# Gather and scatter in turns, a last stage opened by four DMAs, and two operations one slot later

## The chip, the cores and the metric

The kernel runs on one core of one Trainium2 chip. The metric is the device time in microseconds (us) of one execution. The core has TensorE (PE; its weight loads are listed apart as PEld), VectorE (DVE), ScalarE (ACT), GpSimd (POOL) and SyncE (SP), which only issues DMAs here. Each has its own instruction stream, and they meet at semaphores.

## The reference

Two transformer layers over x of shape [8, 512, 128] (4096 tokens), each sublayer followed by a normalisation without weights. What the change touches is the end of the first layer and all of the second:

```python
def _moe_forward(x, router_w, w_gate, w_up, w_down, ws_gate_up, ws_down):   # T=4096, E=64, K=8, C=64
    topk_w, topk_ids = jax.lax.top_k(softmax(x @ router_w.T), K)
    # every expert takes its first C=64 (token, choice) pairs
    xb = x_buf[:E * C].reshape(E, C, -1)
    h = silu(einsum('ecd,edf->ecf', xb, w_gate)) * einsum('ecd,edf->ecf', xb, w_up)
    y = einsum('ecf,efd->ecd', h, w_down).reshape(E * C, -1)
    routed = segment_sum(y[safe] * weight, tok, num_segments=T)
    return routed + silu(sg) * su @ ws_down

x = _layernorm(x + _L0_ffn_ref(x, ...))     # "r": 8 routed rows of a token are added, then normalised
x = _layernorm(x + _L1_attn_ref(x, ...))    # "a": normalises again, gated attention in groups of 32
x = _layernorm(x + _L1_ffn_ref(x, ...))     # "f": 8 experts, each on all tokens, top 2 weights; "t": its output
```

## The kernel before, in words

**First stage** (class `StageA`): for the 8 sequences in turn, attention, MLP and the router's logits. It writes the rows of all tokens, 128 features and 64 router weights each, to the DRAM table `token_rows`. Then DVE picks each expert's 64 tokens (`cand`, `slot_key`), while PE, ACT and POOL compute the shared expert of all tokens, and SP loads the late experts' weights.

**Expert stage** (in `build`): 32 turns `m`, each for two experts of 64 slots. All engines have it unrolled:
- POOL gathers the rows of 128 slots with one indirect DMA (`rows_all`, L1504). All 32 gathers stand ahead of all 32 scatters; from the ninth on each waits for the landing of the gather eight earlier.
- PE transposes them (L1680), ACT copies the transpose (`xgT`, L1590), PE does gate and up (`expert_up`, L1424), ACT the Silu (`sil`, L1406), DVE the product (`hexp`, L1635), PE the down projection (`expert_down`, L1434), DVE multiplies by the router weight into `y_all` (`expert_weigh`, L1414, drawn under the name `x1T_all`, whose memory it uses) and signals `y_sb`.
- POOL scatters the 128 result rows to the DRAM tensor `routed_rows` with one indirect DMA per turn (L1508), which waits for `y_sb`. `rows_scattered` counts landed scatters.

**Opening of the last stage** (class `StageC`). When all scatters have landed, SP loads the eight rows of each token of sequence 0, 2048 KB, with one DMA (`load_contrib`, L814) into `c`. DVE adds 1024 columns down to 128 in three steps over all four token blocks (L1011 to L1015), adds the shared part (`base_all`, L1018), and takes mean and variance (`stats`, L1000 and L1005). POOL then computes, one after another, rstd (add eps, a power, L827 and L829), y minus mean (L885), `x2` (L888), and from rstd the second factor `rq` (L891 to L897, the last a power). ACT makes `z` from `x2` and `rq` (L986), and PE starts on it. Meanwhile POOL corrects the weights `w1n` (L840 to L845: subtract the last column, put the bias there), PE transposes them (L1199), ACT rounds them to `w1_hi` (L915) and DVE keeps the rest in `w1_lo` (L1025).

**Last stage.** `bodies` (L780) runs ten passes. In a full pass, sequence `r` is summed, `a` gets its attention, `f` its eight experts, and `t` its output. A pass has sixteen slots `q`, in each of which PE does six matmuls of 512 columns for the experts (`up`), ACT a sigmoid (`sig`) and DVE a product (`unit`), and every second slot POOL adds one expert (`add_expert`, L837). `up(q)` waits for `unit(q-2)`. The rest stands in a slot by the table `AT`: within a slot it comes behind `up`, `sig` or `unit`. Seven passes have both `a` and `f`. At the end of `a`: `w` (output projection, slot 9) → statistics → rstd on POOL → `x3` (DVE, slot 10) → `x3T` (four transposes on PE, L1303; copies `x3h` on ACT and `x3l` on DVE) → `lg` (twelve small matmuls: the gating logits) → eleven small steps on DVE (`gating`, spread by the table `GATING`), which give the weights `comb` of the next pass.

## Time and profile before

| | |
|---|---|
| Time, median of 3 runs | 766.56 us (765.02 to 769.19) |
| Profiled execution, its own time | 763.75 us |
| Its span in the profile | 762.0 us |
| PE busy | 608.1 us, 80% of the span |
| PEld busy | 477.7 us, 63% |
| DVE busy | 432.4 us, 57% |
| POOL busy | 417.3 us, 55% |
| ACT busy | 276.7 us, 36% |
| Expert stage, first gather to last scatter landed | 186.2 to 299.3 us |
| Last stage | 299.3 to 762.0 us |

Busy shares are means over stages that have little in common. In the expert stage all engines work on small pieces and hand them round; in the full passes of the last stage PE is busy nine tenths of the time. The granted clock of TensorE is 0.5 in the one (the lower of its two levels, 1.2 of 2.4 GHz) and mostly 1.0 in the other. An idle time is worth reading by what ended it: the part behind `<-` in a row. "remote" there means that no instruction of another engine that the profile shows released it at that moment, and "issue" that the engine waited for nothing that is shown.

### The profile page before, as it was taken

The page shows a single profiled execution, that of the slowest core. Times are in us where ns is not written, and L with a number is a line of the kernel's source. Part 1 is how long each engine was busy: PE and PEld are TensorE (multiplying, and loading weights), DVE is VectorE, ACT ScalarE, POOL GpSimd, SP SyncE. Part 2 cuts the span into 40 slices and gives each one's busy share as a digit, 9 for nine tenths or more (in the row PEclk, how much of TensorE's full clock was granted, in tenths as well). Part 3 has the DMA queues.
Part 4 walks back from the last instruction along what each step waited for, and adds up shares of the span by engine and source line. Part 5 has one row for each costly group of instructions (what it writes and reads, how often), then busy time and mean ns, then how long its engine had stood idle before and what let it go on. Part 6 is the DMA issues. An engine that isn't in the chain of part 4 may idle for free.

```text
span 762.0 us, 10293 instructions
## 1 busy us (share of the span) xinstructions
PE 608.1 (80%) x3267; PEld 477.7 (63%) x3267; DVE 432.4 (57%) x1436; ACT 276.7 (36%) x561; POOL 417.3 (55%) x406
## 2 busy tenths in 40 slices
PE   5999995781516997276989989979899898998873
PEld 4888984341405875255777767757677677776652
DVE  2466786796103442633566766656657666575562
ACT  3456653251101222241525426235244362361320
POOL 5453352186773446625366665874857658434371
PEclk9999997595555555567899999999989999799996
DMA  4886755590320003330020210300303000000000
GB/s 113 193 294 249 283 223 233 140 234 11 80 79 25 32 29 104 141 111 1 18 93 1 77 48 1 125 1 0 124 0 105 19 1 15 0 15 1 0 15 14
DMA packets 46901, 61.89 MB, mean 81 GB/s; under 512 B 12835, under 2 KB 39556, under 8 KB 45828
## 3 DMA queue, kind: packets, MB, share of 16 engines
q1 hardware_dynamic: 44292, 56.08, 23.1%
q0 software_dynamic: 2560, 5.23, 2.4%
q8 instruction: 22, 0.36, 0.2%
q14 instruction: 27, 0.22, 0.1%
HBM read 35.10 MB, written 24.13 MB: 78 GB/s over the span
## 4 chain that ended last, share of the span: by engine, by line
PE 44%; DVE 21%; ACT 8%; issue 7%; POOL 6%; another core or an unknown queue 5%; DMA 3%; SPq 0%; DVEq 0%; POOLq 0%; ACTq 0%
PE pair L1189 5%; PE pair L1424 5%; PE pair L1191 5%; PE pair L1190 4%; DVE c_g L1058 3%; POOL c_acc L837 3%; DVE cand L1612 2%; PE pair L1434 2%; DVE keyT L1614 2%; PE pair L1297 2%; ACT c_sg L929 2%; PE pair L1284 2%; PE pair L1289 1%; PE pair L1680 1%
## 5 line engine op out<-in xcount | busy, mean ns | idle before, releaser
L837 POOL TENSOR_TENSOR c_acc<-c_acc,c_g 128x1024 f32<-128x1024 f32 x56 | 133.2, 2379 | 91.0 <-DVE c_g L1058 90.3
L1058 DVE SCALAR_TENSOR_TENSOR c_g<-pair,c_comb,c_sg 128x256 f32<-128x256 f32 x224 | 96.5, 475 | 65.9 <-ACT c_sg L929 63.6
L929 ACT ACTIVATE c_sg<-pair 128x512 f32<-128x512 f32 x128 | 76.1, 595 | 156.3 <-PE pair L1191 156.3
L1189 PE MATMUL pair<-c_w_hi,c_x3h 128*128 128x512 f32 x256 | 113.4, 443 | 7.5 <-DVE c_g L1058 6.2
L1190 PE MATMUL pair<-c_w_lo,c_x3h 128*128 128x512 f32 x256 | 104.5, 408 | 0.0
L1191 PE MATMUL pair<-c_w_hi,c_x3l 128*128 128x512 f32 x256 | 104.4, 408 | 0.0
L1189 PEld LDWEIGHTS pair<-c_w_hi,c_x3h 128*128 128x128 f32 x256 | 50.4, 197 | 24.4 <-DVE c_g L1058 14.9
L1191 PEld LDWEIGHTS pair<-c_w_hi,c_x3l 128*128 128x128 f32 x256 | 50.5, 197 | 12.3
L1190 PEld LDWEIGHTS pair<-c_w_lo,c_x3h 128*128 128x128 f32 x256 | 50.8, 198 | 7.9
L1508 POOL DMA_INDIRECT routed_rows<-x1T_all,dest_row x32 | 31.4, 982 | 40.4 <-DVE x1T_all L1414 37.8
L1635 DVE TENSOR_TENSOR hexp<-sil,pair 96x128 f32<-96x128 f32 x32 | 9.1, 284 | 67.5 <-ACT sil L1406 46.8
L1504 POOL DMA_INDIRECT rows_all<-token_rows,tok_row x32 | 30.5, 955 | 13.2 <-issue 9.4
L859 POOL TENSOR_TENSOR c_c<-c_c 128x2048 f32<-128x2048 f32 x7 | 32.0, 4576 | 0.3 <-DMA c_c<-routed_rows 0.3
L1424 PEld LDWEIGHTS pair<-xgT,wgu_late 128*96 128x96 f32 x160 | 30.1, 287 | 0.3 <-issue 0.3
L1414 DVE TENSOR_SCALAR x1T_all<-pair,rows_all 64x128 f32<-64x128 f32 x64 | 22.4, 350 | 11.4 <-remote 6.4
L1424 PE MATMUL pair<-xgT,wgu_late 128*96 128x64 f32 x160 | 28.8, 361 | 0.0
L1406 ACT ACTIVATE sil<-pair 96x128 f32<-96x128 f32 x32 | 8.7, 273 | 54.0 <-remote 27.0
L827 POOL TENSOR_TENSOR c_rs_f<-c_mv_f,c_eps 128x4 f32<-128x4 f32 x8 | 1.6, 202 | 45.4 <-DVE c_mv_f L1005 45.4
L1045 DVE SCALAR_TENSOR_TENSOR c_gateT<-pair,c_bcols,c_sgt 128x512 f32<-128x512 f32 x16 | 12.0, 749 | 24.7 <-ACT c_sgt L923 24.7
L1434 PE MATMUL pair<-wd_early,hexp 96*64 96x128 f32 x48 | 8.3, 448 | 22.1 <-issue 22.1
L1590 ACT COPY xgT<-pair 128x128 f32<-128x128 f32 x32 | 8.5, 265 | 47.3 <-PE pair L1680 33.5
L1424 PE MATMUL pair<-xgT,wgu_early 128*96 128x64 f32 x96 | 17.5, 364 | 9.1 <-ACT xgT L1590 7.0
(336 smaller groups left out, 1513.5 us busy)
## 6 DMA issues: line engine op xcount, KB each, us to landing
routed_rows<-rows_all SPq DMA_DIRECT2D x8, 2048.0 KB
c_c<-routed_rows SPq DMA_DIRECT2D x8, 2048.0 KB, 8.1
token_rows<-a_xw SPq DMA_DIRECT2D x8, 384.0 KB, 3.3
a_x<-in_L_attn_x SPq DMA_DIRECT2D x8, 256.0 KB, 3.1
base_all<-a_xw SPq DMA_DIRECT2D x8, 256.0 KB, 3.8
out<-c_outb SPq DMA_DIRECT2D x8, 256.0 KB, 5.4
wgu_late<-in_L_ffn_w_gate SPq DMA_DIRECT2D x4, 480.0 KB, 7.8
wgu_late<-in_L_ffn_w_up SPq DMA_DIRECT2D x4, 480.0 KB, 8.3
```

Source lines behind the costliest of these rows:

```text
L837: g.tensor_tensor(acc, acc, b[f"g{e % 2}"][:, :, :], ALU.add).then_inc(s["acc"], 1)
L859: g.tensor_tensor(c[:, :, 0:512], c[:, :, 0:512], c[:, :, 512:1024], ALU.add).then_inc(s["sum_step"], 1)
L929: a_.activation(b[f"sg{q % 2}"][:, :, :], self.pair[q % 2][:, :, H1:2 * H1], SIG).then_inc(s["sig"], 1)
L1058: ins = v.scalar_tensor_tensor(out=dst[:, j, :], in0=self.pair[q % 2][:, x, 0:H1], scalar=b[f"comb{uf}"][:, j * E1 + e:j * E1 + e + 1], in ...
L1189: t.matmul(dst, w_hi, x_hi, start=start, stop=False)
L1190: t.matmul(dst, w_hi, x_lo, start=False, stop=False)
L1191: return t.matmul(dst, w_lo, x_hi, start=False, stop=stop)
L1414: ins = nc.vector.tensor_scalar(y_all[part, m * D:(m + 1) * D], bank[4 + m % 2][part, 0:D], w, None, ALU.mult)
L1424: ins = nc.tensor.matmul(bank[2 + m % 2][0:F0, gu * P + h * CAP:gu * P + (h + 1) * CAP], wgu[:, h, gu, :], xgT[m % 2][:, h * CAP:(h + 1) * ...
L1434: ins = nc.tensor.matmul(bank[4 + m % 2][h * CAP:(h + 1) * CAP, 0:D], hexp[m % 2][:, h * CAP:(h + 1) * CAP], wd[:, h, :], start=True, stop ...
L1504: g.indirect_dma_start(rows_all[:, m * ROW:(m + 1) * ROW], None, table, bass.IndirectOffsetOnAxis(ap=tok_row[:, m:m + 1], axis=0)).then_in ...
L1508: g.indirect_dma_start(contrib, bass.IndirectOffsetOnAxis(ap=dest_row[:, m:m + 1], axis=0), y_all[:, m * D:(m + 1) * D], None, bounds_chec ...
```

## The change

Six edits:

1. The scatters are issued in turns with the gathers: eight gathers, then from turn 8 on gather `m` and scatter `m-8`, then the last eight scatters (`AHEAD = 8`).
2. The correction of `w1n` moves on POOL from behind the scatters to a place ahead of `setup_pool_scale`, before the experts; PE's transposes of it no longer wait for it turn by turn.
3. The first sequence's rows come in four DMAs of 512 KB, one per block of 128 tokens, each with its own semaphore, and DVE sums each block as it lands. Four of the eight `w1_lo` products go ahead of the sums, four behind the statistics.
4. `z` no longer hangs on `x2`: POOL computes `rq` and `nm` (minus mean times `rq`) directly from mean and variance, and ACT makes `z` from `y` with scale and bias. `x2` is computed behind that, and DVE's `w` slot waits for it. POOL waits for the last `z` before it writes `y` anew.
5. The load of sequence `r+1` waits for `y` of the first sequence instead of the third sum (one small addition later than the third sum).
6. `x3T` moves from slot 11 to 12, `lg` from 12 to 13, and the eleven gating steps from 2, 3, 3, 3 in slots 12 to 15 to 4, 4, 3 in slots 13 to 15.

```diff
-AT = dict(..., x3=10, x3T=11, lg=12, y=7, z=11)
-GATING = {12: (1, 2), 13: (3, 4, 5), 14: (6, 7, 8), 15: (9, 10, 11)}
+AT = dict(..., x3=10, x3T=12, lg=13, y=7, z=11)
+GATING = {13: (1, 2, 3, 4), 14: (5, 6, 7, 8), 15: (9, 10, 11)}
...
+    def setup_pool_w1(self, pool):
+        g, k, chain = self.nc.gpsimd, self.k, self.pool_chain
+        pool.wait_ge(self.w1_loaded, 16)
+        chain(g.tensor_copy(k["w127"][:, :], k["w1n"][:, :, D - 1]))
+        for q in range(4):
+            c = slice(8 * q, 8 * q + 8)
+            ins = g.tensor_tensor(k["w1n"][:, c, 0:D - 1], k["w1n"][:, c, 0:D - 1], bcast_last(k["w127"][:, c], D - 1), ALU.subtract)
+        chain(ins)
...
         sp.wait_ge(self.rows_scattered, 16 * EP)
-        self.load_contrib(sp, 0)
+        for j in range(NT):
+            sp.dma_start(self.b["c"][:, j, :], self.contrib_view[0][:, j, :]).then_inc(self.first_part[j][0], 16)
...
             if r is not None:
-                rstd("r", n, "rz_step", 7 * r + 1, "rz_step")
-                g.tensor_tensor(y3d, y3d, bcast_last(mv[:, :, 0], D), ALU.subtract).then_inc(s["rz_step"], 1)
...
+                pool.wait_ge(s["mv_r"], r + 1)
+                g.tensor_tensor(rs, var, k["eps"][:, :], ALU.add).then_inc(s["rz_step"], 1)
+                g.tensor_scalar(rq, var, 1.0 + EPS, EPS * EPS, ALU.mult, ALU.add).then_inc(s["rz_step"], 1)
+                g.tensor_scalar(nm, mean, -1.0, None, ALU.mult).then_inc(s["rz_step"], 1)
+                pool.wait_ge(s["rz_step"], 7 * r + 2)
+                g.tensor_tensor(rq, rq, k["mhalf"][:, :], ALU.pow).then_inc(s["rz_step"], 1)
+                pool.wait_ge(s["rz_step"], 7 * r + 4)
+                g.tensor_tensor(nm, nm, rq, ALU.mult).then_inc(s["rz_step"], 1)
+                g.tensor_tensor(rs, rs, k["mhalf"][:, :], ALU.pow).then_inc(s["rz_step"], 1)
+                g.tensor_tensor(x2, y3d, bcast_last(mean, D), ALU.subtract).then_inc(s["rz_step"], 1)
+                pool.wait_ge(s["rz_step"], 7 * r + 7)
+                g.tensor_tensor(x2, x2, bcast_last(rs, D), ALU.mult).then_inc(s["x2"], 1)
...
-                    act.wait_ge(s["rz_step"], 7 * r + 7)
-                    act.wait_ge(s["x2"], r + 1)
+                    act.wait_ge(s["rz_step"], 7 * r + 5)
...
+        dve.wait_ge(self.rows_scattered, 16 * EP)
+        for q in range(4):
+            w1_low(q)
...
+        for j in range(NT):
+            dve.wait_ge(*self.first_part[j])
+            v.tensor_tensor(c[:, j, 0:512], c[:, j, 0:512], c[:, j, 512:1024], ALU.add).then_inc(s["first_sum"], 1)
...
-            for m in range(EP):
+            def gather(m):
...
-            for m in range(EP):
+            def scatter(m):
...
+            for m in range(EP + AHEAD):
+                if m < EP:
+                    gather(m)
+                if m >= AHEAD:
+                    scatter(m - AHEAD)
```

On POOL in the expert stage, before: `rows_all<-token_rows` is a gather, `routed_rows<-x1T_all` a scatter.

```order
L1504 DMA rows_all<-token_rows,tok_row 128x192 x7
L1504 DMA rows_all<-token_rows,tok_row 128x192 [waits gathered0]
L1504 DMA rows_all<-token_rows,tok_row 128x192 [waits gathered1]
...
L1504 DMA rows_all<-token_rows,tok_row 128x192 [waits gathered7]
L1508 DMA routed_rows<-x1T_all,dest_row 32768x128 [waits y_sb] x32
L840 COPY c_w<-c_w1n 128x32 [waits c_w1_loaded]
```

And now:

```order
L1523 DMA rows_all<-token_rows,tok_row 128x192 x7
L1523 DMA rows_all<-token_rows,tok_row 128x192 [waits gathered0]
L1528 DMA routed_rows<-x1T_all,dest_row 32768x128 [waits y_sb]
L1523 DMA rows_all<-token_rows,tok_row 128x192 [waits gathered1]
L1528 DMA routed_rows<-x1T_all,dest_row 32768x128 [waits y_sb]
L1523 DMA rows_all<-token_rows,tok_row 128x192 [waits gathered2]
L1528 DMA routed_rows<-x1T_all,dest_row 32768x128 [waits y_sb]
```

From the tenth gather on, each now stands behind a scatter, and so behind a wait for the experts' results.

On POOL behind the first statistics of the last stage, before (`c_y` is y, `c_x` is `x2`):

```order
L827 TENSOR_TENSOR c_rs_r<-c_mv_r,c_eps 128x4 [waits c_mv_r,c_pad]
L829 TENSOR_TENSOR c_rs_r<-c_rs_r,c_mhalf 128x4 [waits c_rz_step]
L885 TENSOR_TENSOR c_y<-c_y,c_mv_r 128x512
L888 TENSOR_TENSOR c_x<-c_y,c_rs_r 128x512 [waits c_rz_step]
L891 TENSOR_TENSOR c_rq<-c_rs_r 128x4
L893 TENSOR_TENSOR c_rq<-c_rq,c_mv_r 128x4 [waits c_rz_step]
L895 TENSOR_TENSOR c_rq<-c_rq,c_eps 128x4 [waits c_rz_step]
L897 TENSOR_TENSOR c_rq<-c_rq,c_mhalf 128x4 [waits c_rz_step]
```

And now:

```order
L893 TENSOR_TENSOR c_rs_r<-c_mv_r,c_eps 128x4 [waits c_mv_r]
L894 TENSOR_SCALAR c_rq<-c_mv_r 128x4
L895 TENSOR_SCALAR c_nm<-c_mv_r 128x4
L897 TENSOR_TENSOR c_rq<-c_rq,c_mhalf 128x4 [waits c_rz_step]
L899 TENSOR_TENSOR c_nm<-c_nm,c_rq 128x4 [waits c_rz_step]
L900 TENSOR_TENSOR c_rs_r<-c_rs_r,c_mhalf 128x4
L901 TENSOR_TENSOR c_x<-c_y,c_mv_r 128x512
L903 TENSOR_TENSOR c_x<-c_x,c_rs_r 128x512 [waits c_rz_step]
```

ACT's `z` waited for the eighth of these rows and waits for the fifth now; the two wide ones are last.

On PE in a full pass around slot 12, before. `pair0` and `pair1` are the buffers of `up` in even and odd slots, `c_x30` is `x3`, `c_wg_hi` the first weight of the logits.

```order
L1191 MATMUL pair1<-c_w1_hi,c_x3l1 128x512
L1303 MATMUL pair3<-ident,c_x30 128x128 [waits c_x3]
L1303 MATMUL pair3<-ident,c_x30 128x128 x3
L1208 REGISTER_ALU
L1189 MATMUL pair0<-c_w1_hi,c_x3h1 128x512 [waits c_g]
...
L1191 MATMUL pair0<-c_w1_hi,c_x3l1 128x512
L1189 MATMUL pair3<-c_wg_hi,c_x3h0 128x8 [waits c_x3l]
```

And now:

```order
L1205 MATMUL pair0<-c_w1_hi,c_x3l1 128x512
L1318 MATMUL pair3<-ident,c_x30 128x128 [waits c_x3]
L1318 MATMUL pair3<-ident,c_x30 128x128 x3
L1221 REGISTER_ALU
L1203 MATMUL pair1<-c_w1_hi,c_x3h1 128x512 [waits c_g]
...
L1205 MATMUL pair1<-c_w1_hi,c_x3l1 128x512
L1203 MATMUL pair3<-c_wg_hi,c_x3h0 128x8 [waits c_x3l]
```

The six matmuls of slot 12 (`pair0`) stand ahead of the transposes now, and those of slot 13 (`pair1`) ahead of the logits.

## Rows read from the trace of the kernel before

**Rows 1.** Windows of the kernel before: busy time (and count) of each engine, clock, DMA.

```profile
218.00:222.00 4.00, 0.00 (x0) 0.00 (x0) 0.00 (x0) 0.00 (x0) 3.09 (x4) 0.50 0.31 82
...
238.00:294.00 56.00, 56.00 (x324) 44.95 (x323) 24.29 (x75) 13.19 (x49) 24.86 (x26) 0.50 0.09 30
...
456.00:504.00 48.00, 43.97 (x236) 34.55 (x234) 32.28 (x111) 20.64 (x40) 32.92 (x23) 1.00 0.15 50
...
504.00:555.00 51.00, 46.15 (x226) 36.56 (x227) 31.79 (x112) 20.26 (x38) 33.10 (x23) 0.92 0.14 47
```

**Rows 2.** Timeline of the expert stage: start, length, engine, operation, [idle <-releaser].

```profile
187.78 0.95 POOL L1504 DMA_INDIRECT rows_all<-token_rows,tok_row  x1 [0.30 <-issue]
...
194.23 0.71 DVE L1414 TENSOR_SCALAR x1T_all<-pair,rows_all 64x128 f32<-64x128 f32 x2
...
205.91 0.27 ACT L1406 ACTIVATE sil<-pair 96x128 f32<-96x128 f32 x1 [6.73 <-remote]
...
209.79 1.54 PE L1424 MATMUL pair<-xgT,wgu_early 128*96 128x64 f32 x8 [2.13 <-issue]
...
226.97 0.27 ACT L1406 ACTIVATE sil<-pair 96x128 f32<-96x128 f32 x1 [17.23 <-remote]
...
229.15 0.98 POOL L1508 DMA_INDIRECT routed_rows<-x1T_all,dest_row  x1 [0.30 <-issue]
...
235.37 0.27 ACT L1590 COPY xgT<-pair 128x128 f32<-128x128 f32 x1 [8.13 <-remote]
...
291.39 0.98 POOL L1508 DMA_INDIRECT routed_rows<-x1T_all,dest_row  x1 [1.28 <-DVE x1T_all L1414]
...
297.03 0.98 POOL L1508 DMA_INDIRECT routed_rows<-x1T_all,dest_row  x1 [0.30 <-issue]
```

**Rows 3.** A queue of the page's part 3: packets, MB, share of 16 engines.

```profile
q8 instruction: 22, 0.36, 0.2%
```

**Rows 4.** Timeline of the opening of the last stage.

```profile
299.31 29.41 SPq L814 DMA_DIRECT2D c_c<-routed_rows  x3
...
307.95 2.29 DVE L1011 TENSOR_TENSOR c_c<-c_c 128x2048 f32<-128x2048 f32 x1 [12.24 <-DMA c_c<-routed_rows]
...
312.26 0.69 DVE L1018 TENSOR_TENSOR c_y<-c_y,base_all 128x512 f32<-128x512 f32 x1
...
314.00 0.28 DVE L1005 BATCH_NORM_AGGREGATE c_mv_r<-c_st_r 128x2 f32<-128x6 f32 x3
...
314.70 1.05 POOL L829 TENSOR_TENSOR c_rs_r<-c_rs_r,c_mhalf 128x4 f32<-128x4 f32 x1
...
317.86 0.20 POOL L891 TENSOR_TENSOR c_rq<-c_rs_r 128x4 f32<-128x4 f32 x1
...
318.69 1.01 POOL L897 TENSOR_TENSOR c_rq<-c_rq,c_mhalf 128x4 f32<-128x4 f32 x1
...
319.79 1.28 ACT L986 ACTIVATE c_z<-c_x,c_rq 128x128 f32<-128x128 f32 x4 [0.68 <-POOL c_rq L897]
```

**Rows 5.** Timeline of GpSimd: the wait ahead of the experts, one w1n subtraction.

```profile
148.01 1.90 POOL L727 TENSOR_SCALAR c_whqk<-c_whqk,c_cols 128x640 f32<-128x640 f32 x1 [17.34 <-ACT c_bcols L776]
...
298.35 1.03 POOL L844 TENSOR_TENSOR c_w1n<-c_w1n,c_w 128x508 f32<-128x508 f32 x1
```

**Rows 6.** Waits of TensorE from 186 to 762 us: total, times, longest.

```profile
PE pair L1303 <- DVE c_x L1035: 19.7, 8, 4.9
```

**Rows 7.** Timeline of one pass of the last stage, at its end.

```profile
501.22 0.17 DVE L1074 MAX8 c_top<-pair 128x8 f32<-128x8 f32 x1
...
506.96 0.39 PE L1190 MATMUL pair<-c_w_lo,c_x3h 128*128 128x512 f32 x1
...
507.19 0.39 PE L1191 MATMUL pair<-c_w_hi,c_x3l 128*128 128x512 f32 x1
...
507.44 2.37 POOL L837 TENSOR_TENSOR c_acc<-c_acc,c_g 128x1024 f32<-128x1024 f32 x1 [0.96 <-DVE c_g L1058]
...
509.87 0.66 PE L1244 MATMUL pair<-ident,c_acc 128*128 128x128 f32 x4 [0.45 <-POOL c_acc L837]
```
## What the change was predicted to do

> **What bounds the kernel now.** I read the windows first: they show where no engine works. In the expert stage there is such a stretch: from 218 to 222 us PE, PEld, DVE and ACT did nothing at all, while POOL was busy with four gathers [rows 1]. From 238 to 294 us the same stage has PE busy for 56.00 of 56.00 us at clock 0.50 [rows 1]: there PE sets the pace. The full passes of the last stage are the third kind: PE 43.97 of 48 us at clock 1.00 [rows 1].
>
> Next I read the timeline of the expert stage, for what ends the idle time. POOL issues a gather every 1.25 us (0.95 busy, 0.30 between), from 186.5 us on, 32 of them, so to about 226.5 [rows 2]. The first turn's result is ready at 194.94 (194.23 + 0.71) [rows 2]. But then ACT comes late. A Silu starts at 205.91 after 6.73 us of idling; the matmuls that feed the next one end at 211.33, and it starts at 226.97, 15.6 us late and half a microsecond after the last gather. POOL then issues three scatters, the last until 230.13, and ACT is late once more, until 235.37 [rows 2]. All these rows say "remote": nothing that another engine did released ACT. From 235.4 on nobody is late any more, although scatters go on, one per 2.26 us (0.98 busy, 1.28 waiting for DVE) [rows 2]. So the pauses go with indirect DMAs issued without a gap, and about 36 us of the stage were spent in them. What the waiting engines lack is most probably their next instructions: they are the only thing outside the semaphores that they need, and they travel by DMA too, 22 packets in one queue of the page [rows 3]. A packet there is 16 KB (0.36 MB over 22).
>
> On this the Trainium skill has a rule: "Runtime: NRT & Kernel Launch", section "Instruction fetch mechanics", says that the sequencer streams its code by its own DMA queue and that this is mostly hidden. Packets of 16 KB agree with it; "hidden" does not fit the 15.6 us above, unless these pauses are no fetches. In that case the order of POOL's DMAs would change nothing in them; this is the rival "the pauses stay".
>
> At the opening of the last stage the timeline shows one chain: load issued 299.31, sums from 307.95, last sum ended 312.95, statistics ended 314.28, POOL's eight steps, `z` at 319.79 [rows 4]. In the full passes I read PE's waits: the four transposes of `x3` wait 19.7 us in 8 times, the longest 4.9 [rows 6].
>
> **Expert stage.** Nothing is added or removed on any engine: 32 gathers at 1.25 and 32 scatters at 1.28 us (0.98 + 0.30 [rows 2]), now mixed. POOL issues gathers 0 to 8 back to back, then pairs of 2.53 us. Three pairs later, near 205 us, it needs the result of turn 3. In the trace before, the Silu of that turn starts only at 205.91 [rows 2] (it is the fourth, at one per 2.26 us from the first result). So POOL has to fall silent, and with it the pauses should end, where before it went on for another 21 us. How soon ACT runs freely after that is not shown; the nearest rows give 0.5 us (gathers end, 226.97) and 5.2 us (230.13 to 235.37) [rows 2]. One round would put it at 205.5 to 210; if a scatter and a gather that slip in start the pause anew, two more rounds of 2.53 + 5.2 put it at about 225. I take 213, nearer to the single round. From free running to the last landing it took 299.3 - 235.4 = 63.9 us, set by PE at 2.26 us a turn; POOL's own share of that is 20 pairs and 8 scatters, 50.6 + 10.2 = 60.8 us, so it stays hidden by 3 us. The stage ends 235.4 - 213 = **22 us** earlier. Upper bound: no pause at all, first result 194.94, 31 turns of 2.26, then issue and landing of the last scatter, 3.6 us: 268.6, thus 30 us. Lower bound: the rivals.
>
> **Weights `w1n`.** POOL does the same subtraction, eight pieces of 1.03 us [rows 5], now as four of twice the size, about 8.5 us with a copy, where it waited 17.34 us for ACT [rows 5]. That wait hides it; without it the shared expert would start up to 8.5 us later. Behind the scatters it was beside the load of 8.6 us and cost nothing, so its going brings nothing.
>
> **Opening.** The load takes 8.6 us and the sums 5.0 [rows 4]. With four blocks, three quarters of the sums lie beside the rest of the load, since a block's sums (1.25 us, some 1.4 with four starts) are shorter than a block's share of the time (2.2). Behind the last block 1.4 us are left: **3.6 us** saved. Bounds: 2.6, if three more DMAs delay the last block by a microsecond, and 4. The four `w1_lo` products ahead of it are 2.8 us beside a load whose first block can't be there before.
>
> From the statistics to `z` it is 5.5 us (314.28 to 319.79). The new chain is three small steps, a power, one small step: a small step is 0.28 from start to start (317.86 to 318.69 are three), the power 1.05 [rows 4]. That is 2.2, with handing over 2.3: **3.2 us** saved, bounds 2.8 and 3.4. The wide steps to `x2` go behind it; they are needed at slot 9 of the next pass. The four `w1_lo` products behind the statistics (2.8 us) end before `zh` is there, and PE waits for them only at its first `up`. Both kept waits on `z` (POOL before it writes y, a slot-11 event of the pass before) find it long done: nothing. In later passes `z` was no one's last wait, so the shorter chain brings nothing there.
>
> **The slots.** Without the 4.9, the transposes wait 14.8 us in 7 passes, 2.1 each [rows 6]. Now PE has `up(12)` to do meanwhile: six matmuls at 0.23 us (506.96 to 507.19 [rows 7]), 1.39 us. `x3` is not later, so the logits end at the same instant as before (DVE reads them at 501.22 [rows 7]), with PE one slot further. What follows is the chain logits → gating → last products → POOL's last add at 507.44 → transposes of `acc` at 509.87 [rows 7]: 6.2 us from the logits to the add, in which three products of DVE stood; one of them is now ahead. A product is 0.9 us, and the gating steps in fewer slots give some of it back or not. I take **1.0 us** a pass, 7 in all. Bounds: 1.39 a pass (9.7), and minus 0.7 (-5) if the batches of four steps hold up products that PE waits for.
>
> **Clock.** The pass of 504 to 555 us took 51 us at a mean clock of 0.92 against 48 at 1.00 [rows 1]. PE stood still longest at the transposes; with a third of that gap left I expect fewer drops, and take **2 us**, between -3 and 6.
>
> **Sum.** 22 + 3.6 + 3.2 + 7 + 2 = 37.8 us off the profiled execution of 763.75 us: 726.0. The median of the runs is 2.8 above that execution, so 728.8; I say **728 us**. Half a per cent, 3.8 us, is about what a measurement of this kernel can tell from no change.
>
> **The rivals.**
> - *No pause at all* (chance 0.16): 30 us in the stage, 46 in all: 720 to 721; with the slots and clock at their best, 715. For it: before the third scatter everything is already less dense than before. Against: nine gathers still come without a gap, and the first late Silu lies right behind them.
> - *The pauses come back* (0.16): a pair of gather and scatter takes POOL 2.53 us where PE needs 2.26 a turn, so the indirect DMAs are again nearly without a gap, for 50 us instead of 40. Each time an engine needs code, it waits until POOL has run out of results, 5 to 7 us. Two or three more such pauses take 14 us back: 743.
> - *The pauses stay* (0.07): they hang on the place in the program, not on the gathers. The stage ends as before, 16 us are left: 751.
> - *The slots cost* (0.06): gating in fewer slots makes PE wait 1 us a pass more: 14 us less than forecast, 743.
> - *Slower* (0.07): fetches creep as long as any gather is in the queue, and now gathers last until the end. POOL then goes at the pace of pair plus quiet time, for 24 pairs. It decides against the change from 4.5 us a pair on: from 198 us, 24 x 4.5 and 10 us of last scatters and landing give 316, 17 later than before, which uses up the 16 us of the rest. At 5.6 us a pair the stage ends at 342, 43 us later: 794; at 2.53 + 5.2 it would be far more. Against it: scatters alone, 1.28 us apart from the next, did no harm.
>
> **How the numbers follow.** The forecast has 0.48, its own range is 722 to 737. The time holds in 715 to 750 about 8 times in 10 or a little more: it takes in every case but the slower one and some strays. Faster by over 0.5%: all but the last rival and 0.02 of others, 0.91; the same 0.02; slower 0.07.
>
> **What would show it.** Timeline of the expert stage: POOL's first gap near 205 us, ACT free by 210 to 216, no four-microsecond window without PE afterwards, the four first loads issued near 277. From the load's issue to the statistics' end 11.4 us instead of 15.0; from there to `z` 2.3 instead of 5.5. PE's waits: the transposes near 0.7 us a pass. The forecast is wrong if ACT's late starts go on behind 225 us, or if a full pass takes more than 47 us at clock 1.00.

## The result, and the profile after

| | before | after |
|---|---|---|
| Time, median of 4 runs each | 765.79 us (761.14 to 769.19) | 737.38 us (733.70 to 739.81) |
| Ratio | | 0.9629, 95% interval 0.9558 to 0.9700 |
| Profiled execution, span, mean clock | 763.75, 762.0, 0.845 | 739.48, 737.4, 0.862 |
| Until the first gather | 186.2 | 187.8 (+1.6) |
| First gather to first load of the last stage | 113.1 | 102.4 (-10.7) |
| That load to `z` | 20.5 | 14.1 (-6.4) |
| `z` to the first transposes of `x3` | 35.9 | 38.2 (+2.3) |
| First to last transposes | 345.3 | 335.1 (-10.2) |
| Last transposes to the end | 61.0 | 59.9 (-1.1) |

The change makes the kernel faster, inside the range of 715 to 750, 0.4 us outside the forecast's own 722 to 737, and 9 us short of 728: it saves 28.4 us by the medians and 24.6 in the profiled spans, where 37.8 were forecast. Most of the missing part, 11.3 us, lies in the expert stage. First its timeline after the change:

```profile
207.88 1.02 POOL L1528 DMA_INDIRECT routed_rows<-x1T_all,dest_row  x1 [3.10 <-DVE x1T_all L1429]
...
214.94 0.70 PE L1449 MATMUL pair<-wd_early,hexp 96*64 96x128 f32 x4
...
215.57 0.48 PE L1706 MATMUL pair<-ident,rows_all 128*128 128x128 f32 x1
...
219.41 0.71 DVE L1429 TENSOR_SCALAR x1T_all<-pair,rows_all 64x128 f32<-64x128 f32 x2 [2.24 <-PE pair L1449]
219.44 0.27 ACT L1616 COPY xgT<-pair 128x128 f32<-128x128 f32 x1 [2.59 <-PE pair L1706]
...
223.00 0.27 ACT L1421 ACTIVATE sil<-pair 96x128 f32<-96x128 f32 x1 [3.29 <-remote]
223.31 0.28 DVE L1661 TENSOR_TENSOR hexp<-sil,pair 96x128 f32<-96x128 f32 x1 [3.18 <-issue]
...
226.67 1.02 POOL L1528 DMA_INDIRECT routed_rows<-x1T_all,dest_row  x1 [3.41 <-DVE x1T_all L1429]
...
277.24 0.98 POOL L1528 DMA_INDIRECT routed_rows<-x1T_all,dest_row  x1 [2.85 <-DVE x1T_all L1429]
```

GpSimd falls silent at 204.8 us, as forecast, until 207.88. But then it happens again, every 18.8 us: at 226.67, at 245 and 264, and at 277.24. The long pauses of before (ACT idles 17.2 us ahead of the Silu at 226.97 [rows 2]) have become many short ones. The rows also show who is late. At 219.4 DVE and ACT start within 0.03 us of each other. Each engine has one such instruction per turn, so they can be paired by counting turns: this is DVE's product of turn 7 and ACT's copy of turn 10. DVE's matmuls ended at 215.64 (214.94 + 0.70), ACT's at 216.05: 3.77 and 3.39 us earlier. Yet `hexp`, which waits for ACT, starts 0.04 us after `sil` has ended (223.27 to 223.31). Only starts that wait for **TensorE** are late.

The same pairing corrects a reading of the prediction. The Silu at 226.97 in the kernel before is that of turn 4 (the fifth), and its matmuls are not those that end at 211.33, which are turn 5's, but these:

```profile
199.24 1.54 PE L1424 MATMUL pair<-xgT,wgu_early 128*96 128x64 f32 x8
...
206.56 0.70 PE L1434 MATMUL pair<-wd_early,hexp 96*64 96x128 f32 x4 [5.78 <-issue]
207.18 0.48 PE L1680 MATMUL pair<-ident,rows_all 128*128 128x128 f32 x1
```

They end at 200.78, so the Silu is 26.2 us late, not 15.6. And while that signal was under way, TensorE itself went on: its next groups start 0.06 us behind `hexp` (ended 206.50) and 0.05 us behind `xgT` (209.74, then 209.79 [rows 2]). Nor did instructions arrive in that time. All that the DMA engines moved from 195 to 236 us, in which ACT started late six times (last at 226.97 and 235.37), is GpSimd's queue (packets, MB, share of 16 engines); the next packet of an instruction queue comes at 236.6:

```profile
q0 software_dynamic: 1348, 2.75, 24.9%
```

I count a start on ACT or DVE as late when it lies over 0.5 us behind the end of its own turn's matmuls; a start in order lies 0.02 to 0.05 us behind. Before there are 12 such, 156 us in sum, the longest 27.7; after 38, 142 us in sum, the longest 7.2 (one that only stands behind a late one in its engine's order is counted too). The sum hardly fell; it was spread over the stage, and partly hidden by the turns in hand. In both traces, and in those of all the experiments, the waits for TensorE end in the order in which its matmuls ended, whichever engine waits.

The expectations below were written with another count, which sets a start against the latest matmuls of its kind that had begun, often those of the turn after its own. It gives 8 late starts with 53 us before and 22 with 44 after; where a forecast of theirs is judged, I give that count too.

The opening of the last stage:

```profile
290.18 1.77 SPq L811 DMA_DIRECT2D c_c<-routed_rows  x4
...
293.63 0.69 DVE L1026 TENSOR_TENSOR c_c<-c_c 128x512 f32<-128x512 f32 x1 [0.97 <-DMA c_c<-routed_rows]
...
301.62 0.28 DVE L1010 BATCH_NORM_AGGREGATE c_mv_r<-c_st_r 128x2 f32<-128x6 f32 x3
...
302.83 1.05 POOL L897 TENSOR_TENSOR c_rq<-c_rq,c_mhalf 128x4 f32<-128x4 f32 x1
...
304.25 1.65 ACT L991 ACTIVATE c_z<-c_y,c_nm,c_rq 128x128 f32<-128x128 f32 x4 [10.24 <-POOL c_nm L899]
```

The first sum starts 3.5 us behind the load's issue instead of 8.6 [rows 4]. Statistics end at 301.90, 11.7 us behind the issue; `z` follows 2.35 us later. TensorE's waits (total, times, longest) and two stretches between transposes (windows: busy time of PE, PEld, DVE, ACT, POOL, then clock, DMA share, GB/s):

```profile
PE pair L1318 <- DVE c_x L1048: 6.9, 8, 5.0
PE pair L1259 <- POOL c_acc L853: 9.9, 8, 4.0
```

The second of them was, before:

```profile
PE pair L1244 <- POOL c_acc L837: 7.6, 8, 4.0
```

```profile
434.00:482.00 48.00, 45.31 (x238) 34.98 (x236) 33.15 (x118) 21.71 (x41) 33.58 (x24) 1.00 0.14 50
482.00:534.00 52.00, 47.96 (x236) 37.28 (x235) 33.14 (x117) 21.50 (x40) 33.37 (x24) 0.93 0.13 46
```

Without the first 5.0, the transposes wait 1.9 us in seven passes, where it was 14.8 [rows 6]. Part of that moved: the transposes of `acc` wait 2.3 us longer. A pass with the clock at 1.00 throughout takes 47.6 us, against 48.35 before. The mean clock of the stretch 482 to 534 us is 0.93, and it took 51.9 us; before, three of the seven took 51.0 to 52.3.

### The profile page after: what moved, and what is told of

It is laid out like the page before. It is cut to its first block, busy times and chain, and to the rows that moved or that the text cites. A ratio compares the mean times of both kernels' runs of the same rounds, so it can differ in the third digit from the quotient of the medians.

```text
span 737.4 us, 10292 instructions
## 1 busy us (share of the span) xinstructions
PE 608.2 (82%) x3267; PEld 474.0 (64%) x3267; DVE 436.7 (59%) x1448; ACT 279.2 (38%) x561; POOL 418.7 (57%) x395
## 4 chain that ended last, share of the span: by engine, by line
PE 46%; DVE 22%; issue 9%; ACT 8%; POOL 6%; DMA 2%; another core or an unknown queue 1%; DVEq 0%; POOLq 0%; SPq 0%; ACTq 0%
PE pair L1203 6%; PE pair L1439 5%; PE pair L1205 4%; PE pair L1204 4%; DVE c_g L1071 4%; POOL c_acc L853 3%; PE pair L1449 3%; DVE cand L1638 3%; DVE keyT L1640 2%; PE pair L1312 2%; ACT c_sg L935 2%; PE pair L1706 2%; PE pair L1299 2%; PE pair L1304 1%; PE pair L467 1%
## 5 line engine op out<-in xcount | busy, mean ns | idle before, releaser
L1204 PE MATMUL pair<-c_w_lo,c_x3h 128*128 128x512 f32 x256 | 103.0, 402 | 0.0
L1205 PE MATMUL pair<-c_w_hi,c_x3l 128*128 128x512 f32 x256 | 102.9, 402 | 0.0
L1528 POOL DMA_INDIRECT routed_rows<-x1T_all,dest_row x32 | 32.4, 1012 | 27.7 <-DVE x1T_all L1429 19.9
L220 POOL TENSOR_TENSOR a_rstd<-a_var,a_eps 128x8 f32<-128x8 f32 x8 | 1.6, 205 | 36.2 <-issue 24.9
L1449 PE MATMUL pair<-wd_late,hexp 96*64 96x128 f32 x80 | 13.9, 448 | 9.5 <-issue 6.4
```

Source lines behind the costliest of these rows:

```text
L1204: t.matmul(dst, w_hi, x_lo, start=False, stop=False)
L1205: return t.matmul(dst, w_lo, x_hi, start=False, stop=stop)
L1449: ins = nc.tensor.matmul(bank[4 + m % 2][h * CAP:(h + 1) * CAP, 0:D], hexp[m % 2][:, h * CAP:(h + 1) * CAP], wd[:, h, :], start=True, stop ...
L1528: g.indirect_dma_start(contrib, bass.IndirectOffsetOnAxis(ap=dest_row[:, m:m + 1], axis=0), y_all[:, m * D:(m + 1) * D], None, bounds_chec ...
```

## The experiments

Times are medians, with the ratio to the kernel before, run on the same chip. "Stage" is from the first gather to the issue of the first load; late starts are counted as above, by their own turn's matmuls, in the profiled execution.

| kernel | time | ratio, 95% | before there | stage | late starts, sum |
|---|---|---|---|---|---|
| after | 737.4 | 0.963 (0.956 to 0.970) | 765.8 | 102.4 | 38, 142 us |
| all gathers first | 748.0 | 0.977 (0.972 to 0.981) | 765.8 | 114.7 | 10, 159 us |
| turns only | 756.3 | 0.990 (0.987 to 0.993) | 765.8 | 102.5 | 37, 141 us |
| old slots | 754.3 | 0.987 (0.984 to 0.989) | 765.8 | 103.5 | 39, 149 us |
| spaced DMAs | 767.2 | 1.003 (1.000 to 1.006) | 765.8 | 134.0 | none |
| half rows | 738.4 | 0.963 (0.957 to 0.968) | 766.4 | 102.9 | 46, 144 us |
| three ahead | 761.8 | 0.995 (0.992 to 0.999) | 766.4 | 129.7 | none |
| one load | 737.7 | 0.964 (0.960 to 0.968) | 766.4 | 101.9 | 48, 153 us |
| transposes early | 743.3 | 0.972 (0.967 to 0.976) | 766.4 | 102.2 | 35, 138 us |
| four ahead | 726.6 | 0.986 (0.982 to 0.991) | 736.7 | 94.4 | none |
| five ahead | 722.9 | 0.981 (0.974 to 0.987) | 736.7 | 88.4 | none |
| six ahead | 718.9 | 0.979 (0.974 to 0.984) | 736.7 | 86.2 | none |
| six ahead, again | 730.5 | 0.958 (0.953 to 0.963) | 764.6 | 99.0 | 51, 140 us |

**All gathers first**: the changed kernel with the old order of gathers and scatters.

```diff
-AHEAD = 8
+AHEAD = 32
```

> The changed kernel with AHEAD = 32: all 32 gathers ahead of all 32 scatters again, the rest as changed. If the turns alone carry the stage's gain (10.7 us from the first gather to the last landing in the two traces, 113.1 to 102.4), this runs 9 to 12 us slower than the changed kernel, near 748, and its stage again takes about 113 us with ACT's late starts up to 15 us until the last gather. If the place in the program (instruction fetch) made the pauses and the gain came from elsewhere, it is within 3 us of the changed kernel.

748.0 us against 737.4: the turns are worth 10.6 us here. The stage takes 114.7 us, and its late starts are few and long again, the longest 32.6 us.

**Turns only**: the kernel before with the new order and nothing else.

```diff
+            for m in range(EP + 8):
+                if m < EP:
+                    gather(m)
+                if m >= 8:
+                    scatter(m - 8)
```

> The kernel before with only the turns of gather and scatter. Turns worth 9 to 12 us: 754 to 757 against 766, five pauses of POOL of about 3.4 us waiting for results, late starts of ACT about 6 us behind each resumption. Were the pauses fetches at fixed places of the code, they would come at the same turns as in the changed kernel too, so this run alone does not part the two; it parts the gain of the turns from that of the opening.

756.3 us, 9.5 below the kernel before, with the same stage as the full change. From both sides the turns give 10 us, half of the 22 forecast.

**Spaced DMAs**: a small memset on GpSimd, waited for, behind every indirect DMA.

```diff
+                g.memset(filler[:, :], 0.0).then_inc(s_["filled"], 1)
+                fills[0] += 1
+                pool.wait_ge(s_["filled"], fills[0])
```

> The changed kernel with a memset of 0.5 us on POOL behind every gather and every scatter, so that the indirect DMAs start 1.8 to 1.9 us apart instead of 1.3. Theory A (what follows TensorE comes late because indirect DMAs are issued without a gap): no late starts at all any more, POOL never waits in its pairs, the stage takes 8 x 1.9 + 24 x 3.7 + 8 x 1.9 = 119 us, 17 longer than in the changed kernel, total about 754. Theory F (instructions are fetched at fixed places of the code, in a queue shared with the gathers): fetches still come at the same turns; pauses stay at turns 3, 10, 17, 24, 29 and add to it. Third possibility: it needs more than 0.5 us of gap, then late starts remain and grow rarer.

No start is late any more, with the same instructions at the same places of every other engine's program. The stage takes 134.0 us and the time is 767.2, where theory A had 119 and 754. The timeline shows it: matmuls end at 230.56 and `sil` starts at 230.59.

```profile
229.12 1.44 PE L1440 MATMUL pair<-xgT,wgu_late 128*96 128x64 f32 x8
230.36 0.98 POOL L1526 DMA_INDIRECT rows_all<-token_rows,tok_row  x1 [0.27 <-POOL filler L1536]
...
230.59 0.27 ACT L1422 ACTIVATE sil<-pair 96x128 f32<-96x128 f32 x1 [0.96 <-PE pair L1440]
...
232.71 1.02 POOL L1534 DMA_INDIRECT routed_rows<-x1T_all,dest_row  x1 [0.83 <-POOL filler L1528]
...
234.54 0.98 POOL L1526 DMA_INDIRECT rows_all<-token_rows,tok_row  x1 [0.27 <-POOL filler L1536]
```

The DMAs now start 1.8 to 2.4 us apart, a pair takes 4.2 us, and this costs more than the late starts did. So lateness goes with the density of the indirect DMAs, and does not hang on places in the program. By itself this run leaves the prediction's own theory standing, fetches that dense DMAs hold up: they would be freed here as well. Against that stand the rows above, TensorE on time and no instruction packet in 41 us.

**Half rows**: each gather fetches 64 rows instead of 128, so the kernel leaves half of the experts' inputs out.

```diff
-                g.indirect_dma_start(rows_all[:, m * ROW:(m + 1) * ROW], None, table,
-                                     bass.IndirectOffsetOnAxis(ap=tok_row[:, m:m + 1], axis=0)).then_inc(gathered[m % 8], 16)
+                g.indirect_dma_start(rows_all[0:CAP, m * ROW:(m + 1) * ROW], None, table,
+                                     bass.IndirectOffsetOnAxis(ap=tok_row[0:CAP, m:m + 1], axis=0)).then_inc(gathered[m % 8], 16)
```

> The changed kernel, with every gather fetching 64 of its 128 rows (the other half of the row buffer is zero, so half of the tokens' rows are left out of the experts' inputs); the number of indirect DMAs, their order and the scatters of 128 rows stay. Theory A1 (TensorE's ends reach ACT and DVE late by the number of indirect DMAs that GpSimd issues close together, whatever their rows): the late starts stay, some 30 with a sum of 45 to 60 us, the expert stage stays at 100 to 103 us and the time at 735 to 739. Theory A2 (it goes by rows, that is by descriptors): a turn has 192 rows instead of 256, late starts add up to under 40 us, the stage is 6 to 10 us shorter, time 728 to 732. In either, if GpSimd's 0.95 us of a gather goes by rows, it falls to about 0.5 us and its turn from 2.6 to 2.15 us: that alone is hidden where GpSimd waits for DVE's results.

Late starts are not fewer: 46 with 144 us in sum (by the expectation's count 39 with 74 us, where A2 had under 40 us), and time and stage are those of the changed kernel, as A1 said. GpSimd's groups of gathers (count, busy time, mean ns), first after, then with half the rows:

```profile
L1523 POOL DMA_INDIRECT rows_all<-token_rows,tok_row x32 | 31.3, 980 | 13.2 <-issue 8.8 <-DVE tok_row L1655 3.7 <-DVE x1T_all L1429 0.6
```

```profile
L1524 POOL DMA_INDIRECT rows_all<-token_rows,tok_row x32 | 29.6, 925 | 13.2 <-issue 9.4 <-DVE tok_row L1656 3.7
```

Half the rows save 0.055 us of 0.98: what an indirect DMA costs here, on GpSimd and in late starts, goes by their number and hardly by their rows.

**Three ahead.**

```diff
-AHEAD = 8
+AHEAD = 3
```

> The changed kernel with three gathers ahead of the scatters instead of eight: scatter m now has to wait for the results of a gather issued only three turns earlier, so GpSimd idles a little in every turn instead of 3.4 us in every seventh. Theory A (late ends by dense indirect DMAs): with a turn of 3.0 to 3.4 us no start is late by over 1 us, or under 8 of them, and the stage takes 97 to 106 us: between 731 and 741 us, no pause of 3 us on GpSimd. Rival (eight ahead are needed to hide the gathers' 2 us of landing and the chain of six handoffs): a turn takes over 3.6 us, the stage over 115 us, and the time is over 750.

Both halves of the question have an answer. No start is late, as theory A says; but a turn takes 4.0 us, the stage 129.7 us, and the rival's bound of 750 us holds. GpSimd waits for results in 19 turns:

```profile
POOL routed_rows L1528 <- DVE x1T_all L1429: 44.8, 19, 4.7
```

From a gather to the scatter of its rows it is 14.5 us in the middle of the stage: three turns of 4.0 and some 2.5 us more between the last gather and the scatter; three ahead can't cover that. (The 12.3 us of the expectations below is only the three turns.) Here, too, a gather follows a scatter by 1.3 us, but then 1.9 or 3.5 us pass: what counts is how dense they are over several, not one distance.

**Four, five and six ahead** (`AHEAD = 4`, `5`, `6`).

> The changed kernel with four gathers ahead instead of eight. With three ahead no start was late, but a turn was bound by the way of one turn's rows through the engines, from gather to scatter 12.3 us: 4.1 us a turn. Theory A (late ends come of two indirect DMAs every 2.6 us): at four ahead a turn takes 12.3 / 4 = 3.1 us, the stage 8 x 1.25 + 24 x 3.1 + some 10 = 95 to 100 us, no or few late starts (a sum under 15 us), and the time is 731 to 737 us, up to 6 below the changed kernel. Rival (3.1 us a turn is dense enough as well): late starts add up to over 30 us, the stage takes 102 us or more, the time is 738 to 748.

> The changed kernel with five gathers ahead. Theory A: 12.3 / 5 is below GpSimd's own 2.6 us a turn, so GpSimd is the bound and issues as densely as with eight ahead, until a late end stops it; with less in hand it stops sooner, for shorter times. Late starts add up to 20 to 50 us, the stage takes 98 to 104 us, time 734 to 741. Rival (late ends depend on gathers far ahead, not on density): late starts under 10 us, stage under 97, time under 733.

> The changed kernel with six gathers ahead. Theory A: as with eight, late starts of 40 to 60 us in sum, a stage of 100 to 104 us, time within 3 us of the changed kernel's 737.4. Rival: as for five ahead, under 733 us.

All three were run together, and there the kernel before took 736.7 us, 29 less than elsewhere. None of the three has a late start. Their stages fall from 94.4 to 88.4 and 86.2 us. At four ahead a turn takes 2.7 us in the middle of the stage, not the 3.1 of the expectation, so there already it is nearly GpSimd's own pace of 2.6. At six the stage is that pace: 26 pairs of 2.60, six gathers and six scatters of 1.28 are 83 us, and the landing of the last makes 86. Theory A had expected late starts at five and six, and what came is the rival's none and under 733 us, so either these numbers do not make them or this chip does not. The last run tells the two apart for six; whether four or five ahead would start late on a chip like the others was not run.

**Six ahead, again.**

> The kernel with six gathers ahead once more, with the kernel before beside it. In the last comparison the kernel before took 736.7 us, 30 less than in every other, and no start was late although GpSimd issued an indirect DMA every 1.3 us: either that comparison's chip gives no late ends at all, or six ahead give none. If the kernel before takes about 766 us beside this run: theory A (late ends by dense indirect DMAs, on the chips where they occur) expects late starts of 30 to 60 us in sum again, an expert stage of 98 to 103 us and 733 to 738 us, as with eight ahead; rival (with six ahead the DMAs in hand are few enough) expects none, a stage of 86 us and 718 to 723 us. If the kernel before takes about 737 us again, the run only repeats 718.9 us.

Here the kernel before took 764.6 us, and the late starts are back, 51 of them with 140 us in sum (34 with 48 us by the expectation's count). The same code, on the one chip and the other, first where none is late:

```profile
234.64 0.48 PE L1706 MATMUL pair<-ident,rows_all 128*128 128x128 f32 x1 [0.31 <-DMA rows_all<-token_rows,tok_row]
...
235.16 0.27 ACT L1616 COPY xgT<-pair 128x128 f32<-128x128 f32 x1 [1.14 <-PE pair L1706]
235.82 1.02 POOL L1528 DMA_INDIRECT routed_rows<-x1T_all,dest_row  x1 [0.30 <-issue]
```

```profile
229.34 0.48 PE L1706 MATMUL pair<-ident,rows_all 128*128 128x128 f32 x1
...
235.73 0.71 DVE L1429 TENSOR_SCALAR x1T_all<-pair,rows_all 64x128 f32<-64x128 f32 x2 [1.52 <-PE pair L1449]
236.43 0.27 ACT L1616 COPY xgT<-pair 128x128 f32<-128x128 f32 x1 [2.54 <-PE pair L1706]
...
237.28 1.02 POOL L1528 DMA_INDIRECT routed_rows<-x1T_all,dest_row  x1 [2.56 <-DVE x1T_all L1429]
```

`xgT` starts 0.04 us behind its matmul there, 6.61 here, and GpSimd waits for the result 2.56 us. So the late starts need both, dense indirect DMAs and a chip that has them. The stage with them is 99.0 us, as theory A said for this case, without 86.2; the time is 3 us below its 733 to 738. Of this kernel's 764.6 - 730.5 = 34.1 us, 17.8 remain on the chip without late starts (736.7 - 718.9): if the kernel before has no pauses there either, that is what the opening and the slots give, with whatever the turns give or cost there. Six ahead reaches the best ratio of all to the kernel before, 0.958 against 0.963 for eight, but the intervals overlap and the two weren't run side by side.

**Old slots**: the changed kernel with `x3T`, `lg` and `GATING` as before.

```diff
-AT = dict(..., x3=10, x3T=12, lg=13, y=7, z=11)
-GATING = {13: (1, 2, 3, 4), 14: (5, 6, 7, 8), 15: (9, 10, 11)}
+AT = dict(..., x3=10, x3T=11, lg=12, y=7, z=11)
+GATING = {12: (1, 2), 13: (3, 4, 5), 14: (6, 7, 8), 15: (9, 10, 11)}
```

> The changed kernel with x3T, lg and the gating steps in their old slots. Slots worth 0.75 us in an undisturbed pass (48.35 to 47.6 between the transposes in the two traces) and the rest of the 9 us by clock drops that fell away: 5 us slower if only the slots count (742), 9 to 12 slower if the 2.1 us wait at the transposes also brings the clock drops back (747). Rival: the clock drops are chance and not tied to the wait; then 5 us and some passes at 51 us in either kernel.

754.3 us: the slots are worth 16.9 us, nearly twice the forecast 7 + 2. The first to the last transposes take 350.2 us instead of 335.1. One of its passes (537.5 to 588.7) and what follows the wait at its end:

```profile
537.50:588.70 51.20, 47.16 (x236) 37.49 (x236) 32.69 (x116) 21.36 (x39) 33.17 (x24) 0.93 0.13 46
...
588.00:591.00 3.00, 2.34 (x10) 1.86 (x11) 2.08 (x5) 1.65 (x4) 2.92 (x2) 0.83 0.00 0
591.00:594.00 3.00, 3.00 (x15) 2.90 (x15) 1.26 (x7) 0.96 (x3) 0.97 (x1) 0.50 0.01 3
```

TensorE waits for `x3` until 588.66 (2.24 us), and 1.3 us later its clock falls to the lower level, 0.50, for 6.8 us. Four of its seven waits of 2.2 us are followed by such a fall within 3 us (those that end at 483, 537, 589 and 640 us), and the stretches from there to the next wait take 51.1 to 54.3 us; the two before 483 take 48.4 and 48.7. The kernel before and turns only, with the same slots, show it too, at two and three of seven waits.

**Transposes early**: only the transposes go back, to slot 11; `lg` and the gating stay in 13 to 15.

```diff
-AT = dict(..., x3=10, x3T=12, lg=13, y=7, z=11)
+AT = dict(..., x3=10, x3T=11, lg=13, y=7, z=11)
```

> The changed kernel with the four x3 transposes back in slot 11, the logits and the gating left in slots 13 to 15. With all three back in their old slots the kernel took 754.3 us instead of 737.4. Theory W (it is TensorE's wait of 2.2 us in each full pass for x3, and the falls of its clock that follow such a wait): the wait is back in full, 13 to 17 us in seven passes, the granted clock falls below 0.9 in three to five stretches of the full passes, and the time is 750 to 755. Rival G (it is the logits' and gating's place, which in the old slots hold up DVE's products): the wait comes back, but time stays at 737 to 743.

743.3 us: neither theory's range, though only 0.3 us above rival G's. The wait is back in full (15.4 us in seven passes), and costs 0.7 us a pass: in five of six stretches the transposes stand 48.1 to 48.4 us apart, where the changed kernel has 47.5 to 47.7. But in the profiled execution the clock does not fall behind any of these waits. Over the four runs of each kernel the mean clock is 0.856 to 0.862 here, 0.844 to 0.849 with the old slots, 0.861 to 0.865 in the changed kernel. One pass and what follows its wait:

```profile
533.40:581.80 48.40, 44.12 (x235) 35.05 (x235) 32.72 (x116) 21.36 (x39) 33.22 (x24) 1.00 0.14 49
...
581.00:584.00 3.00, 2.17 (x12) 1.87 (x13) 2.25 (x6) 1.48 (x4) 2.92 (x2) 1.00 0.00 0
584.00:587.00 3.00, 3.00 (x21) 2.71 (x20) 1.75 (x8) 1.73 (x4) 1.17 (x1) 1.00 0.01 3
```

So of the 16.9 us, 5.9 belong to the transposes' slot and 11 to that of the logits and gating; the two kernels' profiles differ from the first to the last transposes by 13.9 us, and in the clock. The wait of 2.2 us alone does not bring the fall: it stood in both kernels. Why the logits one slot later keep the clock up is open.

**One load**: a single DMA of 2048 KB for the first sequence.

```diff
-        for j in range(NT):
-            sp.dma_start(self.b["c"][:, j, :], self.contrib_view[0][:, j, :]).then_inc(self.first_part[j][0], 16)
+        sp.dma_start(self.b["c"][:, :, :], self.contrib_view[0]).then_inc(self.first_part[3][0], 16)
...
-            dve.wait_ge(*self.first_part[j])
+            dve.wait_ge(*self.first_part[3])
```

> The changed kernel with one DMA of 2048 KB in place of the four of 512 KB at the opening of the last stage; DVE's sums, block by block, all wait for it. The forecast's own term: 3.6 us slower (2.6 to 4), so 740 to 742 us, from the load's issue to z 17.7 us instead of 14.1. Rival (the sums were bound by DVE or by the transfer anyway, and the gain of 6.4 us between load and z comes all from the shorter chain to z): within 1 us of the changed kernel.

At its own place the term is right. Three rows of this kernel, and the one of the changed kernel that answers to the last:

```profile
288.68 0.37 SPq L810 DMA_DIRECT2D c_c<-routed_rows  x1
...
306.84 1.26 ACT L990 ACTIVATE c_z<-c_y,c_nm,c_rq 128x128 f32<-128x128 f32 x3 [14.34 <-POOL c_nm L898]
...
310.89 4.54 POOL L866 TENSOR_TENSOR c_c<-c_c 128x2048 f32<-128x2048 f32 x1 [1.05 <-DMA c_c<-routed_rows]
```

```profile
308.60 4.55 POOL L867 TENSOR_TENSOR c_c<-c_c 128x2048 f32<-128x2048 f32 x1 [1.35 <-DMA c_c<-routed_rows]
```

From the load to `z` it is 18.2 us instead of 14.1: 4.1 more. The second sequence's sums start 22.2 us behind the load instead of 18.4, 3.8 more. But the first transposes come 54.2 us behind it instead of 52.3: half is gone. The rest went in the clock: in this execution the clock stood at 1.00 from 354 to 696 us, and its transposes span 331.1 us, not 335.1. The times can't tell the two kernels apart (737.7 and 737.4), so the gain of the four loads is shown in the trace to 2 us, and in the time not at all. For the opening as a whole there is one more pair of runs, beside the same kernel before: old slots (turns and opening) is 11.5 us below it, turns only 9.5.

## Why the prediction was right in its sign and too hopeful

- **Expert stage, 22 us: the step that failed.** "POOL has to fall silent, and with it the pauses should end": it fell silent at 204.8 as said, and the pauses came back. This is the rival "the pauses come back", with half of its mechanism (a pair of 2.6 us is nearly as dense as gathers alone; its other half, engines that need code, is not what happened) and nearly its price: 11.3 us of the 22 were lost, mostly by four more silences of GpSimd, of 2.9 to 3.4 us, where the rival had two or three of 5 to 7. The prediction's own sign of failure, "ACT's late starts go on behind 225 us", was met. That scatters did no harm [rows 2] had misled: they were 2.26 us apart because PE set the pace, not because they were scatters.
- **Its explanation fell too.** Late engines do not lack instructions. ACT and DVE, whose code is separate, are released within 0.03 us of each other, and only where they wait for TensorE; TensorE itself went on in time while its signal was under way; and no instruction packet moved from 195 to 236 us, in which six of ACT's starts were late. The 15.6 us were read against the matmuls of the next turn; it was 26.2. The rule quoted from the Trainium skill ("Runtime: NRT & Kernel Launch", section "Instruction fetch mechanics"), that fetches are mostly hidden, stands: in those 41 us there was no fetch to hide.
- **Without late starts the term would probably have held.** The forecast had the stage at 91 us (113.1 - 22), with an upper bound that gives 83; on the chip without them six ahead took 86.2. Eight ahead was not run there.
- **Opening, 3.6 + 3.2: right at its place.** 11.7 us from load to statistics' end (forecast 11.4), then 2.35 (2.3); 6.4 us in all. Not foreseen: the way from `z` to the first transposes took 2.3 us longer, with more of it at the clock's lower level (0.50 for 24 us of 38.2, before for 17 of 35.9), and the run with one load shows that it absorbs half of what the four loads save.
- **Slots, 7 us: the sign right, the mechanism half.** In an undisturbed pass 0.75 us (forecast 1.0) by 1.9 us of waits instead of 14.8 (forecast 0.7 a pass, measured 0.27). The forecast put the gain down to TensorE's wait at the transposes; the runs give 5.9 us of 16.9 to their slot, and 11 to that of the logits and gating, which it had only as a risk. Its second sign of failure, a full pass over 47 us at clock 1.00, was met as well: 47.6.
- **Clock, 2 us: too small.** First to last transposes gained 10.2 us in the profiled executions, of which 0.75 x 6 + 0.1 = 4.6 by the waits (the first of the seven stretches gained only 0.1); the other 5.6 are fewer falls. Over several runs, the slots and with them the clock are worth 16.9 us.
- **`w1n`: nothing, as said.** GpSimd still waits 10.7 us for ACT behind it. The first gather comes 1.6 us later, but 1.4 of that stand already at 31.5 us, far ahead of that code.

The profiled spans differ by 24.6 us: 10.7 + 6.4 - 2.3 + 10.2 + 1.1 - 1.6 = 24.5. Against 37.8 forecast, 11.3 are the stage, 3.9 the two stretches not foreseen, 0.4 the opening, and 2.3 came back in the passes and behind them. That the total stayed in the range is in part luck: the stage gave about half of its term, and the slots with the clock, by the runs, nearly twice theirs.

## What to carry to other kernels

When an engine starts late, look at whom it waits for before naming what it lacks: that only TensorE's consumers were late, two engines at one instant, was in the trace before any experiment. And pair a start with its own turn's work, not with the nearest. A pause made by one queue's density ends only if the queue becomes less dense than the pace at which it did no harm; moving its DMAs about spreads the pause. And where small matmuls stand in a pass that repeats can be worth more by the clock than by the idle time, so count the falls of the clock too.

## What the runs showed of the hardware

- With an indirect DMA every 1.3 us on GpSimd (0.95 to 1.02 us busy each, 0.30 between), ends of TensorE's matmuls reached ACT and DVE up to 27.7 us late in the kernel before and up to 32.6 with all gathers first, in the order in which the matmuls had ended. What ACT and DVE sent arrived within 0.06 us meanwhile, at each other and at TensorE. At 1.8 us apart and more none was late. Half the rows in each gather did not help: 46 starts were late, against 35 to 48 in kernels with the same order and all rows.
- One of the chips used shows none of this: the kernel before took 736.7 us there, against 764.6 to 766.4 elsewhere. No profile of that kernel was taken there; that its pauses are what is missing is inferred from the three others run beside it. What sets that chip apart is open, as is the way in which the DMAs hold up TensorE's signals.
- An indirect DMA of 64 rows costs GpSimd 0.925 us, one of 128 rows 0.98.
- TensorE's clock fell to its lower level (0.50, 1.2 of 2.4 GHz) for 6.8 us behind a wait of 2.2 us, at four of seven such waits of one kernel, and at none of another with the same waits, in one profiled execution of each.
